# Two attention layers on one NeuronCore, first turn: the last two heads' G in three split passes behind the attention, their operands split during the softmax

## Chip, cores and metric

The kernel runs on one core of one Trainium2 chip. The time is the device time of one execution in microseconds; the median of three runs of the kernel before is 1091.12 us (1090.59 to 1092.88).

## The reference

128 graphs of 64 nodes with 256 features go through two layers. The first is a masked multi-head attention with 8 heads of 32, an output projection and a layer norm. The second is a graph attention with four heads:

```
Wh     = einsum(h, W) + bW            # 4 heads, 256 x 256 each
e      = einsum(Wh, attn)
A_mat  = tanh(where(adj, einsum(e, Wh), 0))
hp     = relu(einsum(A_mat, Wh))
ha, hf = concat(hp) @ A_w.T, h @ fc_w.T
coeff  = sigmoid(hf @ g1_w.T + ha @ g2_w.T + gbias)
out    = layernorm(h + hf * coeff + ha * (1 - coeff))
```

Since W and attn are constant, the scores of a head are h G h^T with G = W^T attn^T W. The kernel computes G once for each head: first M (a product of attn and W), then G from M and W. It also needs W transposed.

## The kernel before

The 128 graphs are 16 groups of 8. A turn takes group A through the first layer and group B = A - 1 through the second, interleaved on each engine; turn 0 has only the first layer of group 0 and the preparation of the weights, and a last turn only the second layer. Turns 2 to 14 are a loop, the others are written out. Each of the five engines has its own list of steps in order (the five functions `turn`); an engine does its steps in that order and waits on semaphores between them. So a step that waits holds everything behind it on its engine. SP issues the loads and stores, PE is TensorE, ACT ScalarE, DVE VectorE and POOL GpSimd.

Precision: most matmuls are made of three passes of fp32r operands. A value is split into `_hi`, a copy rounded to fp32r (made by ACT), and `_lo`, the remainder (a subtraction, made by DVE or POOL); lo x hi, hi x lo and hi x hi are added up in PSUM. M and G are computed in plain fp32 instead, for which the trace shows two rows for each matmul, and each result is split afterwards: `G_high` on ACT (L877), `G_low` on DVE (L1108). M1 holds M in SBUF.

PSUM has eight banks. `claim` makes PE wait until the tile that was in a bank before has been taken; `await_tile` makes a reader wait for a bank to be filled. The lists FIRST, BODY and LAST say which tile goes to which bank: G4 to G6 follow G0 to G2 in banks 1 to 3, G7 follows G3 in bank 6.

Steps of turn 0 that matter here, in order:

- PE (L755): queries, keys, scores, M0 to M7 (L419), values, then the transposes of the probabilities (L542) mixed with G0 to G3 (L431), the attention (L560: 128 small matmuls), G4 to G6, the output projection `project` (L382 to L384), G7, the transposes of W (L441), queries of group 1, the gate weights, the transposes of h (L585), keys of group 1.
- ACT (L1022): the M copies (L871) mixed with three of the four exponentials (L911), wo_hi (`out_weight`, L866), the value copies (L907), the probs copies (L916) and G_high(0 to 3), x_hi of group 1 (`x_split`, L827), at_hi (`attention`, L925), then `late(0)`, `late(1)` and `late(2)` (L858: the rounded parts of A_w in two halves and of g2_w) between G_high(4 to 7), then the W copies.
- DVE (L1367): the softmax (`shift`: mask added L1187, maximum L1190, difference L1192; `total`: sum L1197, reciprocal L1200), wo_lo (`early_low(3)`, L1120), `shifted_fc` (L1146, L1148), G_low, at_lo, `residual`, `new_h` (L1271), h's low part.
- POOL (L1518): the mask, `probs_scaled` (L1480: four products by the reciprocals), `x_and_bias` (L1473: y plus the output bias), x_lo of group 1 (L1441), `late(0)` (L1451: aw_lo, 128 x 2048), `root_1` (the inverse deviation of the first norm), the mask of group 1, `h_low` (L1455), `hT_whole` (L1463), `late(1)` (L1451: the low part of g2_w, called g in the trace).

In turn 1 PE computes T0 to T7 of group 0 (hT times G) with the scores of group 1 behind T0, then half of hf, and then `adj_scores` (L615), which waits until ACT has copied T4 to T7. ACT's order there is T0, T1, exponential 0, T2, T3, exponential 1, T4, T5, exponential 2, T6, T7, exponential 3, hf, tanh. Each exponential waits for DVE's difference L1192 of its tile.

Of the kernel before, what the change touches and what calls it, by code (L numbers as in the profile page):

```python
# [5 lines left out]
F32 = mybir.dt.float32  # L6
F32R = mybir.dt.float32r
# [3 lines left out]
ALU = mybir.AluOpType  # L11
# [3 lines left out]
P = 128  # L15
# [43 lines left out]
def stage_kernel(nc, x, xT, adjS, adjT, masks, eye, pair_eye, wq, bq, wk, bk, wv, bv, wo, bo,  # L59
                 Wn, attn, AwT, fcn, g1T, g2T, gb, out):  # L60
    ctx = ExitStack()
    with ctx:
# [26 lines left out]


        Wq, Wk, Wv, Wo = (pair(n, [P, DC, D]) for n in ("wq", "wk", "wv", "wo"))
        Wt = pair("wt", [P, DC, H2 * D])
        G = pair("g", [P, DC, H2 * D])
        FF = pair("ff", [P, DC, 2 * D])
        Aw = pair("aw", [P, KC, D])
# [63 lines left out]
        raw_m = at("raw_m", [P, JB - 1, S], F32, r_U + 18432)  # L159
        w_sum = at("w_sum", [P, DC * H2], F32, r_U + 19200)  # L160
        w_off = at("w_off", [P, DC * H2], F32, r_U + 19232)
        fc_sum = at("fc_sum", [P, DC], F32, r_U + 19264)
        assert base + place[0] <= nc.sbuf_usable_end, (base, place[0], nc.sbuf_usable_end)

# [34 lines left out]
        passed = sem("passed")  # L199
        zeros_ready, end_ready = sem("zeros_ready"), sem("end_ready")  # L200
        neg2, from2_ready, last_stats = sem("neg2"), sem("from2_ready"), sem("last_stats")

        def carried(eng):

# [175 lines left out]
        def _(pe):  # L380
# [42 lines left out]
            def G_products(ns):  # L423
                if 0 in ns:
                    for n in range(4, 8):
                        await_taken(pe, "S", f"M{n}", 0)
                for n in ns:
                    hh, dc = n // DC, n % DC
                    bank = claim(pe, "S", f"G{n}", 0)
                    for pc in range(DC):  # L430
                        ins = pe.matmul(bank[:, 0:D], M1[:, pc, hh, dc * P:dc * P + P],  # L431
                                        W_nat[:, pc * H2 + hh, 0:D], start=pc == 0, stop=pc == DC - 1)
                    filled(ins, "S", f"G{n}", 0)
# [321 lines left out]
            def turn(A, B, more):  # L755
                if B is None:
                    warm_up()
                    first_queries()
                    keys(0)
                    scores(0)  # L760
                    M1_products(range(H2 * DC))
                    values(0, 0)
                    values(0, 1)
                    probs_T(0, range(2))
                    G_products(range(2))
                    probs_T(0, range(2, 3))
                    G_products(range(2, 3))
                    probs_T(0, range(3, JB))
                    G_products(range(3, 4))
                    attention(0, range(DC))  # L770
                    G_products(range(4, 7))
                    project(0)
                    G_products(range(7, H2 * DC))
                    W_transposed()
                    queries(1)
                    gate_weights()
                    h_T(0)
                    keys(1)
                    return
                for n in range(KC):  # L780
                    T_tile(B, n)
                    if A is not None and n == 0:
                        scores(A)
                    if A is None and n == 3:
                        res_T(B - 1)
                h_fc(B, 0)
                adj_scores(B)
                if A is None:
                    h_fc(B, 1)
                    gathered(B)  # L790
                    for s in range(2):
                        gate_h_half(B, s)
                    heads_out(B, range(KC))
                    h_a_half(B, 0, 0)
                    h_a_half(B, 0, 1)
                    h_a_half(B, 1, 0)
                    gate_a_half(B, 0)
                    h_a_half(B, 1, 1)
                    res_T_first(B)
                    gate_a_last(B)  # L800
                    res_T_last(B)
                    return
                values(A, 0)
                values(A, 1)
                probs_T(A, range(JB))
                gathered(B)
                attention(A, range(DC))
                h_fc(B, 1)
                heads_out(B, range(KC // 2))
                project(A)  # L810
                heads_out(B, range(KC // 2, KC))
                h_a(B)
                gate_h(B)
                h_T(A)
                gate_a(B)
                if more:
                    queries(A + 1)
                    keys(A + 1)
                    res_T(B)
# [4 lines left out]
        def _(act):  # L824
# [29 lines left out]
            def late(n):  # L854

                act.wait_ge(late_in, 16 * 2)
                to, raw = ((Aw[0][:, 0:4, :], raw_A[:, 0:4, :]), (Aw[0][:, 4:8, :], raw_A[:, 4:8, :]), (G2[0][:], raw_g2[:]))[n]
                act.activation(to, raw, ACT.Copy).then_inc(late_hi, 1)  # L858

            def masks_in():  # L860
                act.wait_ge(mask_in, 16)
# [160 lines left out]
            def turn(A, B, more):  # L1022
                if B is None:
# [9 lines left out]
                    M1_copies(range(1, 3))  # L1033
                    exps(0, 1)
                    M1_copies(range(3, 6))
                    out_weight()
                    M1_copies(range(6, H2 * DC))
                    exps(0, 2)
                    values(0, 0)
                    exps(0, 3)  # L1040
                    values(0, 1)
                    probs_T(0, range(2))
# [2 lines left out]
                    G_high(range(2, 3))  # L1045
                    probs_T(0, range(3, JB))
                    G_high(range(3, 4))
                    x_split(1, x_second)
                    attention(0)
                    late(0)  # L1050
                    G_high(range(4, 5))
                    late(1)
                    G_high(range(5, 7))
                    late(2)
                    G_high(range(7, H2 * DC))
                    W_high()
                    queries(1)
                    fc_high()
# [47 lines left out]
        def _(dve):  # L1106
# [37 lines left out]
            def shifted_fc():  # L1144
                dve.wait_ge(gate_in, 16 * 2)
                dve.tensor_reduce(fc_sum[:], fc_nat[:], AX.X, ALU.add).then_inc(sum_fc, 1)  # L1146
                dve.wait_ge(sum_fc, 1)
                dve.scalar_tensor_tensor(out=fc_nat[:], in0=fc_sum[:].unsqueeze(2).to_broadcast([P, DC, D]),  # L1148
                                         scalar=-1.0 / D, in1=fc_nat[:], op0=ALU.mult, op1=ALU.add).then_inc(fc_ready, 1)

            def G_low(ns):
                for n in ns:
# [214 lines left out]
            def turn(A, B, more):  # L1367
                if B is None:
# [4 lines left out]
                    shift(0, 1)  # L1373
                    early_low(2, Wv, raw_v)
                    softmax_rest(0)
                    early_low(3, Wo, raw_o)
                    shifted_fc()
                    G_low(range(4))
                    attention(0)
                    G_low(range(4, 7))  # L1380
                    residual(0)
                    G_low(range(7, H2 * DC))
                    W_low(range(2))
                    new_h(0)
                    W_low(range(2, 4))
# [49 lines left out]
        def _(pool):  # L1435
# [82 lines left out]
            def turn(A, B, more):  # L1518
                if B is None:
# [1 line left out]
                    probs_scaled(0)  # L1521
                    x_and_bias(0)
                    x_low(1, x_second)
                    late(0)
                    root_1(0)
                    mask(1)
                    h_low(0)
                    hT_whole(0)
                    late(1)
                    return  # L1530
                if later(B):
# [74 lines left out]
```

## Time and profile before

| | us |
|---|---|
| median of three runs | 1091.12 |
| lowest, highest | 1090.59, 1092.88 |
| the profiled execution | 1093.31 |
| its span in the trace | 1091.5 |
| PE busy in it | 1081.2 (99%) |
| DVE, ACT, POOL busy | 704.5, 544.9, 290.5 |

The span is what the trace covers; the profiled execution took 1.8 us more than its span. Busy time is summed over the whole span and says how loaded an engine is, not when. In the rows below each time is in microseconds from the span's start. A row of the timeline is a start, a duration, the engine, the source line, the operation with its output and inputs, and how many neighbouring instructions of that kind it merges. The granted clock of TensorE is given as a share of its full 2.4 GHz.

### The profile page before, as it was taken

Reading aid. Unit: us, or ns where it says so; the run is one execution under the profiler, and the core shown is the slowest. Engines: PE = TensorE matmul, PEld = TensorE weight load, DVE = VectorE, ACT = ScalarE, POOL = GpSimd, SP = SyncE. Lnnn points to the kernel's source line nnn. Section 1 sums busy time; section 2 is a strip of 40 time slices with the busy share of each in tenths; the row PEclk is TensorE's granted clock in tenths of the full one; section 3 lists DMA queues with packets and bytes.
Section 4 is the critical chain, followed back from the end, with each engine's and each line's share of the span. In section 5 each row is a group of like instructions: output and inputs, shape, how many; then the busy total and the mean of one; then the engine's idle time right before and its main releaser. Section 6 shows DMA issues by size and latency. Waiting matters only on the chain. (4 is left out here: it accounts for less than half of the span.)

```text
span 1091.5 us, 25444 instructions
## 1 busy us (share of the span) xinstructions
PE 1081.2 (99%) x10102; PEld 908.8 (83%) x10102; DVE 704.5 (65%) x1321; ACT 544.9 (50%) x988; POOL 290.5 (27%) x279
## 2 busy tenths in 40 slices
PE   9999999999999999999999999999999999999998
PEld 7788888888888888788888888888888888878887
DVE  7685766666676575765756666575765757666544
ACT  6563553625446373563635446363562735536252
POOL 2442331232322223322232322223322222312200
PEclk9999999999999999999999999999999999999999
DMA  7000100100010000100100010000100001000000
GB/s 263 3 22 22 41 24 20 41 20 19 22 40 22 20 19 22 40 22 20 41 16 24 22 40 22 20 19 22 40 22 20 26 15 39 22 23 22 1 20 20
DMA packets 26590, 32.60 MB, mean 30 GB/s; under 512 B 4161, under 2 KB 23105, under 8 KB 26177
## 3 DMA queue, kind: packets, MB, share of 16 engines
q1 hardware_dynamic: 26128, 31.93, 8.8%
q8 instruction: 21, 0.34, 0.1%
q10 hardware_dynamic: 432, 0.26, 0.1%
q14 instruction: 9, 0.07, 0.0%
HBM read 23.80 MB, written 8.39 MB: 29 GB/s over the span
## 5 line engine op out<-in xcount | busy, mean ns | idle before, releaser
L972 ACT ACTIVATE cat_hi<-bank 128x512 fp32r<-128x512 f32 x128 | 76.6, 598 | 127.0 <-PE bank L395 127.0
L935 ACT ACTIVATE T<-bank 128x512 f32<-128x512 f32 x128 | 75.0, 604 | 86.5 <-PE bank L395 86.4
L1108 DVE SCALAR_TENSOR_TENSOR cat_lo<-bank,cat_hi 128x512 fp32r<-128x512 f32 x128 | 86.5, 685 | 39.0 <-ACT cat_hi L972 37.0
L390 PE MATMUL bank<-hT_hi,g_lo 128*128 128x512 f32 x256 | 102.6, 401 | 0.0
L383 PE MATMUL bank<-cat_hi,aw_lo 128*128 128x512 f32 (+1 forms) x272 | 102.4, 377 | 0.0
L384 PE MATMUL bank<-cat_hi,aw_hi 128*128 128x512 f32 (+1 forms) x272 | 102.4, 377 | 0.0
L382 PE MATMUL bank<-cat_lo,aw_hi 128*128 128x512 f32 (+1 forms) x272 | 102.4, 377 | 0.0
L1480 POOL TENSOR_TENSOR probs<-probs,den 128x512 f32<-128x512 f32 x64 | 67.6, 1057 | 123.9 <-DVE den L1200 122.7
L391 PE MATMUL bank<-U_hi,wt_hi 128*128 128x512 f32 x256 | 99.8, 390 | 0.0
L391 PE MATMUL bank<-hT_hi,g_hi 128*128 128x512 f32 x256 | 99.8, 390 | 0.0
L390 PE MATMUL bank<-U_hi,wt_lo 128*128 128x512 f32 x256 | 99.8, 390 | 0.0
L1108 DVE SCALAR_TENSOR_TENSOR haT_lo<-bank,haT_hi 128x512 fp32r<-128x512 f32 (+1 forms) x34 | 22.4, 660 | 113.2 <-ACT haT_hi L977 106.1
L1473 POOL TENSOR_TENSOR y<-y,bo_all 128x1024 f32<-128x1024 f32 x16 | 38.9, 2434 | 195.4 <-ACT at_hi L925 195.4
L1108 DVE SCALAR_TENSOR_TENSOR U_lo<-bank,U_hi 128x512 fp32r<-128x512 f32 x128 | 78.0, 680 | 12.9 <-ACT U_hi L966 12.9
L977 ACT ACTIVATE haT_hi<-bank 128x512 fp32r<-128x512 f32 x30 | 17.9, 598 | 125.9 <-PE bank L384 125.9
L395 PE MATMUL bank<-U_lo,wt_hi 128*128 128x512 f32 x256 | 78.9, 389 | 0.0
L395 PE MATMUL bank<-hT_lo,g_hi 128*128 128x512 f32 x256 | 78.8, 389 | 0.0
L966 ACT ACTIVATE U_hi<-bank 128x512 fp32r<-128x512 f32 x128 | 64.4, 629 | 8.8 <-PE bank L638 8.8
L1463 POOL TENSOR_TENSOR hT<-hT_hi,hT_lo 128x1024 f32<-128x1024 f32 x16 | 38.8, 2425 | 108.6 <-DVE hT_lo L1108 108.6
L615 PE MATMUL bank<-T,hT 128*64 128x256 f32 x512 | 58.8, 382 | 0.4 <-ACT T L935 0.4
L383 PEld LDWEIGHTS bank<-cat_hi,aw_lo 128*128 128x128 f32 x272 | 51.2, 188 | 9.4
L382 PEld LDWEIGHTS bank<-cat_lo,aw_hi 128*128 128x128 f32 x272 | 51.2, 188 | 9.4
(203 smaller groups left out, 2753.5 us busy)
## 6 DMA issues: line engine op xcount, KB each, us to landing
y<-in_x SPq DMA_DIRECT2D x16, 512.0 KB, 3.6
out<-res SPq DMA_DIRECT2D x15, 512.0 KB, 3.0
x_raw<-in_xT SPq DMA_DIRECT2D x14, 512.0 KB, 3.4
W_nat<-in_Wn SPq DMA_DIRECT2D x1, 1028.0 KB, 7.8
adjS_u<-in_adjS SPq DMA_DIRECT2D x16, 64.0 KB, 3.0
attn_nat<-in_attn SPq DMA_DIRECT2D x1, 1024.0 KB, 9.0
raw_A<-in_AwT SPq DMA_DIRECT2D x1, 1024.0 KB, 8.9
x_second<-in_xT SPq DMA_DIRECT2D x1, 512.0 KB, 10.9
```

The lines of the kernel that those rows point to most:

```text
L382: pe.matmul(out, asel(a[0]), bsel(b[1]), start=first, stop=False)
L383: pe.matmul(out, asel(a[1]), bsel(b[0]), start=False, stop=False)
L384: return pe.matmul(out, asel(a[0]), bsel(b[0]), start=False, stop=last)
L390: pe.matmul(out, wsel(w[1]), dsel(d[0]), start=first and n == 0, stop=False)
L391: pe.matmul(out, wsel(w[0]), dsel(d[0]), start=False, stop=False)
L395: ins = pe.matmul(out, wsel(w[0]), dsel(d[1]), start=False, stop=last and n == len(terms) - 1)
L615: ins = pe.matmul(bank[b * S:b * S + S, q * D:q * D + D].rearrange("p (h n) -> p h n", h=H2), hT[:, k, first:first + S], T[:, k, :, first: ...
L935: take(act.activation(T[:, n % DC, n // DC, :], bank[:], ACT.Copy), "B", f"T{n}", g)
L966: act.activation(U_hi[:, c, :, first:first + P], bank[:].rearrange("p (h t) -> p h t", h=H2), ACT.Copy).then_inc(U_hi_ready, 1)
L972: act.activation(cat_hi[:, n, :], bank[:], ACT.Relu).then_inc(cat_hi_ready, 1)
L1108: return dve.scalar_tensor_tensor(out=out, in0=bank, scalar=bias, in1=hi.bitcast(F32), op0=op, op1=ALU.subtract)
L1480: pool.tensor_tensor(view, view, den[:, j, :].unsqueeze(2).to_broadcast([P, NG, S]), ALU.mult) \
```

## The change

The changed kernel computes G4 to G7 (heads 2 and 3) as three fp32r passes from split copies of M and W, all four behind the attention and ahead of the projection. The split copies M_part and W_part of the two heads lie in the memory of Wt, which is written later. ACT makes the rounded parts (W's where wo_hi was, M's behind the first value copy), DVE the remainders (`parts_low`, where wo_lo was). wo_hi and wo_lo move behind G_high(3) and G_low(3). On ACT x_hi of group 1 goes behind the attention and `late(0 to 2)` behind G_high(7). On POOL `late(0)` moves from behind x_lo to behind `hT_whole`.

```
@@ memory
-        Wt = pair("wt", [P, DC, H2 * D])
+        r_wt = region(16384)
+        Wt = at("wt_hi", [P, DC, H2 * D], F32R, r_wt), at("wt_lo", [P, DC, H2 * D], F32R, r_wt + 8192)
+        W_part = tuple(at(f"W_part{i}", [P, DC, 2, D], F32R, r_wt + 4096 * i) for i in range(2))
+        M_part = tuple(at(f"M_part{i}", [P, DC, 2, D], F32R, r_wt + 8192 + 4096 * i) for i in range(2))
@@ PE, G_products
+                    if n >= H2:
+                        pe.wait_ge(parts_ready, 2)
+                        for pc in range(DC):
+                            ins = product(bank[:, 0:D], M_part, W_part, lambda t: t[:, pc, hh - 2, dc * P:dc * P + P],
+                                          lambda t: t[:, pc, hh - 2, :], pc == 0, pc == DC - 1)
+                        filled(ins, "S", f"G{n}", 0)
+                        continue
@@ PE, turn 0
                     attention(0, range(DC))
-                    G_products(range(4, 7))
+                    G_products(range(4, H2 * DC))
                     project(0)
-                    G_products(range(7, H2 * DC))
@@ ACT
+            def W_part_high():
+                act.wait_ge(W_ready, H2 * DC)
+                act.activation(W_part[0][:], last_heads(W_nat[:, :, 0:D]), ACT.Copy).then_inc(W_part_hi, 1)
+            def M_part_high():
+                for n in range(4, 8):
+                    await_taken(act, "S", f"M{n}", 0)
+                act.activation(M_part[0][:], M1[:, :, 2:4, :], ACT.Copy).then_inc(M_part_hi, 1)
@@ ACT, turn 0
                     M1_copies(range(3, 6))
-                    out_weight()
+                    W_part_high()
                     M1_copies(range(6, H2 * DC))
                     exps(0, 2)
                     values(0, 0)
+                    M_part_high()
                     exps(0, 3)
...
                     G_high(range(3, 4))
+                    out_weight()
+                    attention(0)
                     x_split(1, x_second)
-                    attention(0)
-                    late(0)
-                    G_high(range(4, 5))
-                    late(1)
-                    G_high(range(5, 7))
-                    late(2)
-                    G_high(range(7, H2 * DC))
+                    G_high(range(4, H2 * DC))
+                    for n in range(3):
+                        late(n)
@@ DVE
+            def parts_low():
+                dve.wait_ge(M_part_hi, 1)
+                dve.tensor_tensor(M_part[1][:], M1[:, :, 2:4, :], M_part[0][:].bitcast(F32), ALU.subtract) \
+                   .then_inc(parts_ready, 1)
+                dve.wait_ge(W_part_hi, 1)
+                dve.tensor_tensor(W_part[1][:], W_nat[:, :, 0:D].rearrange("p (o h) d -> p o h d", h=H2)[:, :, 2:4, :],
+                                  W_part[0][:].bitcast(F32), ALU.subtract).then_inc(parts_ready, 1)
@@ DVE, turn 0
                     softmax_rest(0)
-                    early_low(3, Wo, raw_o)
+                    parts_low()
                     shifted_fc()
                     G_low(range(4))
+                    early_low(3, Wo, raw_o)
                     attention(0)
-                    G_low(range(4, 7))
+                    G_low(range(4, H2 * DC))
                     residual(0)
-                    G_low(range(7, H2 * DC))
@@ POOL, turn 0
                     x_low(1, x_second)
-                    late(0)
                     root_1(0)
                     mask(1)
                     h_low(0)
                     hT_whole(0)
+                    late(0)
                     late(1)
```

## Rows read from the trace of the kernel before

**Rows 1.** The page's busy time by engine (busy us, share of span, instructions).

```profile
PE 1081.2 (99%) x10102; PEld 908.8 (83%) x10102; DVE 704.5 (65%) x1321; ACT 544.9 (50%) x988; POOL 290.5 (27%) x279
```

**Rows 2.** Waits of PE: line, what released it, total us, times, longest.

```profile
PE bank L560 <- issue: 2.1, 1, 2.1
...
PE bank L529 <- issue: 1.0, 1, 1.0
```

**Rows 3.** Timeline of PE, first turn: start, duration, line, operation, count.

```profile
27.50 0.66 PE L542 MATMUL bank<-ident,probs 128*128 128x128 f32 x4
...
28.95 1.17 PE L560 MATMUL bank<-PT,v 64*32 64x64 f32 x96
...
32.23 0.46 PE L560 MATMUL bank<-PT,v 64*32 64x64 f32 x32 [2.10 <-issue]
...
32.62 4.54 PE L431 MATMUL bank<-W_nat,M 128*128 128x256 f32 x12
...
36.81 0.47 PE L382 MATMUL bank<-wo_lo,at_hi 128*128 128x256 f32 x1
...
39.86 1.02 PE L431 MATMUL bank<-W_nat,M 128*128 128x256 f32 x4
...
40.73 1.91 PE L441 MATMUL bank<-ident,W_nat 128*128 128x128 f32 x16
...
47.38 1.04 PE L585 MATMUL bank<-ident,y 128*128 128x128 f32 x8
```

**Rows 4.** Windows: length, busy by engine, then PEclk, DMA share, GB/s (last three).

```profile
29.75:30.00 0.25, 0.25 (x37) 0.21 (x25) 0.15 (x1) 0.25 (x1) 0.25 (x1) 1.00 0.23 66
...
33.50:33.75 0.25, 0.25 (x2) 0.19 (x1) 0.04 (x1) 0.25 (x2) 0.00 (x0) 0.50 0.25 66
```

**Rows 5.** Windows around the low clock, and around the stop near 975.

```profile
32.50:36.50 4.00, 4.00 (x36) 3.16 (x14) 2.08 (x5) 3.66 (x8) 0.31 (x1) 0.57 0.02 6
...
974.00:976.00 2.00, 1.10 (x99) 0.96 (x80) 0.00 (x0) 0.36 (x1) 1.55 (x4) 1.00 0.00 0
```

**Rows 6.** Timeline of ACT, first turn.

```profile
24.08 0.63 ACT L911 ACTIVATE probs<-probs 128x512 f32<-128x512 f32 x1 [1.19 <-DVE probs L1192]
```

**Rows 7.** Timeline of DVE, turns 0 and 1.

```profile
25.58 0.96 DVE L1120 TENSOR_TENSOR wo_lo<-raw_o,wo_hi 128x512 fp32r<-128x512 f32 x1
...
44.94 1.38 DVE L1271 TENSOR_SCALAR y<-y,from,rstd 128x256 f32<-128x256 f32 x4 [0.65 <-POOL from L1492]
...
55.47 1.98 DVE L1192 TENSOR_TENSOR probs<-probs,mx 128x512 f32<-128x512 f32 x1
...
58.81 1.46 DVE L1192 TENSOR_TENSOR probs<-probs,mx 128x512 f32<-128x512 f32 x1
...
62.41 0.69 DVE L1192 TENSOR_TENSOR probs<-probs,mx 128x512 f32<-128x512 f32 x1
```

**Rows 8.** Timeline of POOL, turns 0 and 1.

```profile
22.11 1.04 POOL L1480 TENSOR_TENSOR probs<-probs,den 128x512 f32<-128x512 f32 x1 [1.79 <-DVE den L1200]
...
24.96 2.49 POOL L1480 TENSOR_TENSOR probs<-probs,den 128x512 f32<-128x512 f32 x2 [1.80 <-DVE den L1200]
...
36.65 4.60 POOL L1451 TENSOR_TENSOR aw_lo<-raw_A,aw_hi 128x2048 fp32r<-128x2048 f32 x1 [3.84 <-ACT aw_hi L858]
...
54.51 2.40 POOL L1455 TENSOR_TENSOR h_lo<-y,h_hi 128x1024 fp32r<-128x1024 f32 x1
...
56.86 2.86 POOL L1463 TENSOR_TENSOR hT<-hT_hi,hT_lo 128x1024 f32<-128x1024 f32 x1
...
59.67 1.74 POOL L1451 TENSOR_TENSOR g_lo<-raw_g,g_hi 128x512 fp32r<-128x512 f32 x1
```

**Rows 9.** Timeline of ACT, turn 1.

```profile
63.14 0.63 ACT L911 ACTIVATE probs<-probs 128x512 f32<-128x512 f32 x1 [1.23 <-DVE probs L1192]
...
63.68 1.06 ACT L935 ACTIVATE T<-bank 128x512 f32<-128x512 f32 x2
```

**Rows 10.** Timeline of PE, turn 1.

```profile
65.10 3.67 PE L615 MATMUL bank<-T,hT 128*64 128x256 f32 x32
```

More of the change, by code:

```diff
@@ L201, in stage_kernel @@
         neg2, from2_ready, last_stats = sem("neg2"), sem("from2_ready"), sem("last_stats")
+        W_part_hi, M_part_hi, parts_ready = sem("W_part_hi"), sem("M_part_hi"), sem("parts_ready")
         def carried(eng):
@@ L858, in late, with last_heads @@
                 act.activation(to, raw, ACT.Copy).then_inc(late_hi, 1)
+            def last_heads(t):
+                return t.rearrange("p (o h) d -> p o h d", h=H2)[:, :, 2:4, :]
+            def W_part_high():
[5 more added lines that the diff above has]
+                act.activation(M_part[0][:], M1[:, :, 2:4, :], ACT.Copy).then_inc(M_part_hi, 1)
             def masks_in():
```

## The prediction, made before the changed kernel was run

> **What bounds the kernel now.** I read the page's busy times first: TensorE (PE) is busy for 1081.2 of 1091.5 us, so what counts is when PE stands still, runs at its lower clock, or has less to do [rows 1]. The list of PE's waits then shows how few stops there are: 2.1 us in front of an L560 matmul (attention) and 1.0 us at L529 (scores) are the largest behind the start [rows 2]. The timeline of PE puts the 2.1 us into the first turn: 96 of 128 L560 matmuls, nothing from 30.12 to 32.23, then the other 32; no engine is named as releaser ("issue"), and the only transfer near it is one of 66 GB/s over 29.75 to 30.00, 16 KB, which I take for instructions [rows 3, 4]. Last, the windows give the clock: about half a microsecond after PE resumed it fell from 2.4 to 1.2 GHz and came back at 36.1. The mean granted clock of 32.5 to 36.5 is 0.57 of full: 2 x (1 - 0.57) x 4.0 = 3.4 us at half rate, which cost 1.7 us of PE work [rows 5]. The changed G products ran almost wholly in that stretch.
>
> **G's last four tiles (gain).** Before, each of the eight matmuls of G4 to G7 (two per tile, plain fp32) is two rows of the trace. Twelve rows take 32.62 to 36.81 = 4.19 us, the last four 39.86 to 40.73 = 0.87 us: 5.06 us [rows 3]. Afterwards there are 4 x 2 x 3 = 24 fp32r matmuls of 256 columns, the form of the output projection, whose starts are 0.12 us apart at 2.4 GHz (24 in 3.05 us with the first, slower step) [rows 3]. At 1.2 GHz no such row exists; bounds are 0.12 (no slowing) and 0.24 (all of it), and I take 0.24, since the twelve G rows before took 0.35 us each there and the last four 0.22. With the clock's times moved as below: one matmul at full rate, 14.3 in the 3.4 us at half rate, 8.8 at full rate, 4.6 us in all. Change: -0.5 us (from -2.2 with no slow clock to 0).
>
> **The parts split in the softmax's shadow (loss).** On ACT the 1.05 us copy of W's part takes the place of wo_hi (0.62) among the M copies; the M copy behind it, at 20.00, starts 0.4 us later and is still done when the last M bank comes at 20.86. The copy of M's part fits in the 1.19 us that ACT idled ahead of the exponential at 24.08 [rows 6]. On DVE it is different. DVE and POOL do not overlap when both read two SBUF tensors. wo_lo started at 25.58 and took 0.96 us, where the same form takes 0.69; POOL's probs product takes 1.04 when free (22.11), so the one of 24.96 ended at 26.00, and 0.55 us of DVE work followed. The next POOL product, due at 26.00, ended at 27.45: 1.49 us instead of 1.04 [rows 7, 8]. Now M_part_lo stands where wo_lo stood, with 1024 elements for 512: 2 x 0.55 = 1.1 us from 26.0. POOL's fourth product ends at 26.0 + 1.1 + 1.04 = 28.1 instead of 27.5. PE's last four probs transposes, at 27.50 and in front of G3 and the attention, wait for just this product [rows 3]. Loss: +0.64 us (bounds 0 and 0.7; 0 if the instruction stop behind it ends at a fixed time). W_part_lo comes behind that product (28.1 to 29.2), POOL's y plus bias behind W_part_lo (to 31.6), fc_nat's difference behind that (32.2), G_low(0 to 3) by 33.5. PE reaches G4 at 32.62 + 0.64 = 33.26 and wants G0's bank, free at 32.5, then one more bank per tile: no wait, and its new wait for parts_ready is over at 29.2. wo_lo (34.1) is long ready for the projection.
>
> **G7 ahead of the projection, the moved splits on ACT and POOL (nothing in turn 0).** The projection starts at 37.8 instead of 36.81, so y1 and the DVE, POOL, DVE chain behind it come 1.0 us later: h ready at 47.3 instead of 46.3 [rows 7]. PE gets to h's transposes at 47.38 + 0.14 = 47.5 [rows 3]; 1.06 us of slack become 0.2. The at_hi copies are no later than PE, x_hi of the next turn is done at about 36.1 and x_lo at 38.5, with queries(1) at 42.4 on PE. The Aw and G2 copies (2.8 us on ACT) now fill 38.1 to 40.7, before W0 is there. If the 0.2 us are too little, PE waits for what is missing.
>
> **late(0) on POOL, behind hT_whole (the large loss).** The 4.60 us product aw_lo leaves 36.65, where nothing on DVE needed the port (its work there reads PSUM), and lands behind hT, which ends at 59.7 [rows 8]. h_low, for which SP's next x load waits, and hT stay ahead of it; g_lo and the four probs products of turn 1 stand behind it, the last done by 72.7, before PE's transposes want it. There DVE runs the second turn's softmax. Its L1192 subtraction reads two SBUF tensors. Row 55.47 took 1.98 us and ended 0.54 us after POOL's h_low (54.51 + 2.40 = 56.91); row 58.81 took 1.46 us and ended 0.55 us after hT (59.72); the free ones take 0.69 [rows 7, 8]. So aw_lo, due at 59.67, first waits 0.57 us for that second subtraction (as g_lo did: 1.74 us), and holds until 59.67 + 0.57 + 4.60 = 64.84. The third subtraction, at 62.41, then ends at 65.39 instead of 63.10: +2.3 us [rows 7]. Behind it on ACT queue the exponential (63.14), T6 and T7 (until 64.74), and PE's adjacency scores need T7's copy at 65.10: a slack of 0.36 us [rows 9, 10]. PE stands still for 2.3 - 0.36 = 1.95 us (bounds 0 and 2.5; the upper one if the fourth subtraction, due at 67.7, also loses to a POOL product, A_hi then reaches ACT so late that the copy of v0, which frees the bank of the third probs transpose, costs 0.5 more).
>
> The Trainium skill (SBUF — State Buffer, section "Who interferes with whom") says that the port pair of VectorE and GpSimd is an exclusive lock, held for the whole instruction by whoever issues first. If the port were instead shared by bandwidth, the subtraction would lose about its own 0.55 us, nearly covered by the slack, and the change would cost nothing here. The rows above (1.98 and 1.46 us, each ended by POOL's end) agree with the lock; no row shows a DVE instruction behind one as long as 4.6 us.
>
> **The clock after that stop.** The one stop of 2.1 us was followed by 3.4 us at 1.2 GHz; the stop of 1.0 us near 975 was not (clock 1.00) [rows 2, 5]. 1.95 us is nearest to the first, so I take the fall: +1.7 us (bounds 0 and 1.7).
>
> **Instruction positions.** G4 to G7 issue 16 more PE instructions net, so every later fetch point moves by them. Of the kernel's 32 bursts of short matmuls (scores and attention, 16 each) two held such a stop, of 2.1 and 1.0 us [rows 2]; I take 0, bounds -1.0 (the second stop gone) and +1.0 (one more like it).
>
> Sum: -0.5 + 0.64 + 1.95 + 1.7 = +3.8 us. The profiled execution took 1093.31 us for a span of 1091.5 and would take 1097.1. It lies 2.2 us above the median of the runs, 1091.12; against that median I forecast 1094.9 us.
>
> **Rivals.**
> A. The lock holds but the clock does not fall, since the stop is a little shorter than the one that had that result: -0.5 + 0.64 + 1.95 (to 2.5) = +2.1 to +2.6, 1093.2 to 1093.7. For it: one precedent only on each side. Against: 1.95 is nearly 2.1.
> B. aw_lo does not reach PE: the third subtraction gets in before it, or POOL's order is shifted by a microsecond. Then -0.5 + 0.64 = about 0, 1091.2. Against: POOL's queue is in order and aw_hi has been ready for 20 us.
> C. Faster: the first turn's 2.1 us stop is set by when its instructions arrive and not by when PE gets there. Then the 0.64 us of waiting come out of the stop, which shrinks to 1.5 us, and the clock does not fall (it decides between 1.0 and 2.1). All 24 passes run at 0.12: 2.9 instead of 5.06 us, -2.2. With B's absence of the port stop this gives 1088.9; with the port stop it gives 1090.9 (+1.95, clock full). Against: the fetch appears to follow PE's own progress, since the next 16 KB moved (33.50 to 33.75) 1.4 us after PE had resumed [rows 4].
> D. The change does less than it says: the 24 passes cost no less than the 16 rows (0 instead of -0.5). 1095.4, inside the forecast's own spread.
>
> **How the numbers follow.** Forecast with the clock's fall (D in it) 0.45, A 0.27, B 0.14, C 0.14. A measurement of this kernel can tell 0.2% (2.2 us) from no change, so the borders are 1088.9 and 1093.3. Slower: the forecast's 0.43 and half of A, 0.56. Faster: the better half of C, 0.07. The rest, 0.37, is the same. Range 1090.6 to 1096.0: its top is the forecast with the 0.5 of the v0 copy and 0.6 of a new short stop, its bottom leaves out only half of C and a little of B. The likeliest case alone spans 1093.9 to 1096.0.
>
> **What would show it.** Right: PE idle in front of L615 of about 2 us near 66, released by ACT's T copy; an L1192 row of about 3 us there, beside a POOL aw_lo row of about 5.2; clock 0.50 for some 3 us behind it; probs T3 transposes 0.6 us late; G4 to G7 in one block of 4.6 us. Wrong: an unlengthened third L1192, a clock of 1.00 at 68 to 71 (then A), or an attention stop well under 2.1 us (then C).

## The result

The changed kernel takes 1094.16 us in the median of 17 runs (1092.61 to 1096.91), the kernel before 1090.47 us in 17 runs beside them (1088.35 to 1094.22). The ratio is 1.0039, interval 1.0029 to 1.0049: slower by 4.2 us by the ratio (3.2 to 5.3), and by 3.7 us from median to median. The forecast was +3.8 us, or 1094.9 us. The kernel before spreads over 6 us by itself, and most of that goes with a stop of PE that only some executions have (below); so beside each median the lowest time is of use, since it compares the least disturbed executions: 1092.61 against 1088.35 is +4.3 us.

In the changed kernel the source lines are others: L1223 is L1192 of before (the softmax's subtraction), L628 is L615 (adjacency scores), L573 is L560 (attention), L1482 is L1451 (aw_lo, g_lo), L598 is L585 (h's transposes), L555 is L542 (probs transposes), L387 to L389 are L382 to L384 (the three passes of a product), L1131 is L1108 (the remainders), L413 is L408 (a wait of the last turn that both kernels have), L959 the copies of T (L935).

The list of PE's waits of the changed kernel (total us, times, longest) already holds the answer to [rows 2] (one row of 0.2 us is left out):

```profile
PE bank L628 <- ACT T L959: 2.5, 2, 2.2
PE bank L413 <- POOL hf L1467: 1.3, 1, 1.3
PE bank L387 <- DVE g_lo L1131: 1.3, 1, 1.3
PE bank L555 <- POOL probs L1511: 0.4, 1, 0.4
PE bank L387 <- DVE at_lo L1131: 0.2, 1, 0.2
```

The two stops of before, at attention and at scores of a late turn, are gone from this execution; in their place PE waits 2.2 us for a copy of T, 1.3 us for G_low and 0.6 us in small pieces. The timelines of DVE and POOL in turn 1 show what is behind the first; they answer to [rows 7, 8]:

```profile
53.42 1.99 DVE L1223 TENSOR_TENSOR probs<-probs,mx 128x512 f32<-128x512 f32 x1
...
56.76 1.46 DVE L1223 TENSOR_TENSOR probs<-probs,mx 128x512 f32<-128x512 f32 x1
...
60.36 2.88 DVE L1223 TENSOR_TENSOR probs<-probs,mx 128x512 f32<-128x512 f32 x1
...
65.40 1.53 DVE L1223 TENSOR_TENSOR probs<-probs,mx 128x512 f32<-128x512 f32 x1
```

```profile
52.45 2.41 POOL L1486 TENSOR_TENSOR h_lo<-y,h_hi 128x1024 fp32r<-128x1024 f32 x1
54.80 2.87 POOL L1494 TENSOR_TENSOR hT<-hT_hi,hT_lo 128x1024 f32<-128x1024 f32 x1
57.63 5.06 POOL L1482 TENSOR_TENSOR aw_lo<-raw_A,aw_hi 128x2048 fp32r<-128x2048 f32 x1
62.64 1.73 POOL L1482 TENSOR_TENSOR g_lo<-raw_g,g_hi 128x512 fp32r<-128x512 f32 x1
```

The third subtraction is issued at 60.36, while aw_lo holds the port from 57.63 (its first half microsecond waits for the second subtraction) until 62.69. It ends at 63.24, 0.55 us after that, instead of after 0.69 us. The exponential, T6 and T7 follow it on ACT until 64.87, and PE's scores start at 65.24 with 2.17 us of idle time before them. The windows (last three columns: PEclk, DMA share, GB/s) show that the clock fell to half in this execution: (1 - 0.57) x 2 x 4 = 3.4 us at half rate, the length of [rows 5].

```profile
63.81 1.06 ACT L959 ACTIVATE T<-bank 128x512 f32<-128x512 f32 x2
```

```profile
62.46 0.62 PE L400 MATMUL bank<-hT_lo,ff_hi 128*128 128x512 f32 x2
65.24 5.36 PE L628 MATMUL bank<-T,hT 128*64 128x256 f32 x32 [2.17 <-ACT T L959]
```

```profile
64.00:66.00 2.00, 0.76 (x8) 0.66 (x10) 1.93 (x4) 0.88 (x2) 2.00 (x3) 1.00 0.00 0
66.00:70.00 4.00, 4.00 (x25) 2.85 (x23) 3.60 (x6) 1.71 (x3) 2.42 (x3) 0.57 0.00 0
```

Turn 0 of the same execution, first DVE, then PE. They answer to [rows 3, 7]:

```profile
25.41 1.50 DVE L1176 TENSOR_TENSOR M_part<-M,M_part 128x1024 fp32r<-128x1024 f32 x1
26.82 2.06 DVE L1179 TENSOR_TENSOR W_part<-W_nat,W_part 128x1024 fp32r<-128x1024 f32 x1
28.81 0.67 DVE L1169 TENSOR_REDUCE fc_sum<-fc_nat 128x2 f32<-128x512 f32 x1
29.51 2.15 DVE L1171 SCALAR_TENSOR_TENSOR fc_nat<-fc_sum,fc_nat 128x512 f32<-128x512 f32 x1
31.59 1.41 DVE L1131 SCALAR_TENSOR_TENSOR g_lo<-bank,g_hi 128x256 fp32r<-128x256 f32 x4
```

```profile
26.41 1.03 PE L444 MATMUL bank<-W_nat,M 128*128 128x256 f32 x4
27.86 0.66 PE L555 MATMUL bank<-ident,probs 128*128 128x128 f32 x4 [0.42 <-POOL probs L1511]
...
29.31 1.48 PE L573 MATMUL bank<-PT,v 64*32 64x64 f32 x128
32.05 0.39 PE L387 MATMUL bank<-W_part,M_part 128*128 128x256 f32 x1 [1.26 <-DVE g_lo L1131]
...
34.91 0.28 PE L389 MATMUL bank<-W_part,M_part 128*128 128x256 f32 x1
35.42 0.35 PE L387 MATMUL bank<-wo_lo,at_hi 128*128 128x256 f32 x1 [0.23 <-DVE at_lo L1131]
```

Here all 128 attention matmuls run in one piece, so PE is at G4 at 30.8 and not at 33.3. The bank of G0 is free only when G_low(0) has run, and that stands on DVE behind three instructions that waited for POOL (1.50, 2.06 and 2.15 us where the bare work is 1.1, 1.1 and 0.55). The 24 passes then take 32.05 to 35.03 (the last start and one step of 0.12) = 2.98 us at full clock.

The idle times in brackets are shorter than what a wait costs, since a matmul row lasts beyond the start of the next (the passes are 0.28 us long and start 0.12 us apart). From start to start the costs come out larger. The probs transposes start 1.45 us after the G2 rows ahead of them, where e5 below needs 0.86; G4 starts 2.74 us after the attention, where e9 below needs 1.41; the projection starts 0.51 us after the last pass, instead of 0.12; the scores of L628 start 2.78 us after the last hf rows, and those of the kernel before 0.59. So the four waits cost 0.59, 1.33, 0.39 and 2.19 us, where the brackets say 0.42, 1.26, 0.23 and 2.17. The rows for comparison, of e5, of e9 and of the kernel before:

```profile
26.59 1.03 PE L431 MATMUL bank<-W_nat,M 128*128 128x256 f32 x4
27.45 0.60 PE L542 MATMUL bank<-ident,probs 128*128 128x128 f32 x4
```

```profile
29.41 1.48 PE L573 MATMUL bank<-PT,v 64*32 64x64 f32 x128
30.82 0.38 PE L387 MATMUL bank<-W_part,M_part 128*128 128x256 f32 x1
```

```profile
64.51 0.61 PE L395 MATMUL bank<-hT_lo,ff_hi 128*128 128x512 f32 x2
```

### The profile page after: what moved, and what is told of

It is laid out like the page before. It is cut to its first block and busy times, and to the rows that moved or that the text cites. A ratio compares the mean times of both kernels' runs of the same rounds, so it can differ in the third digit from the quotient of the medians.

```text
span 1092.2 us, 25470 instructions
## 1 busy us (share of the span) xinstructions
PE 1080.7 (99%) x10110; PEld 908.8 (83%) x10110; DVE 713.9 (65%) x1323; ACT 546.7 (50%) x990; POOL 291.2 (27%) x279
## 5 line engine op out<-in xcount | busy, mean ns | idle before, releaser
L959 ACT ACTIVATE T<-bank 128x512 f32<-128x512 f32 x128 | 75.0, 603 | 85.5 <-PE bank L400 85.5
L1131 DVE SCALAR_TENSOR_TENSOR cat_lo<-bank,cat_hi 128x512 fp32r<-128x512 f32 x128 | 86.5, 686 | 39.0 <-ACT cat_hi L996 37.0
L389 PE MATMUL bank<-cat_hi,aw_hi 128*128 128x512 f32 (+1 forms) x272 | 102.6, 377 | 0.0
L387 PE MATMUL bank<-cat_lo,aw_hi 128*128 128x512 f32 (+1 forms) x272 | 102.5, 377 | 0.0
L1131 DVE SCALAR_TENSOR_TENSOR haT_lo<-bank,haT_hi 128x512 fp32r<-128x512 f32 (+1 forms) x34 | 22.4, 660 | 113.1 <-ACT haT_hi L1001 106.0
L1131 DVE SCALAR_TENSOR_TENSOR U_lo<-bank,U_hi 128x512 fp32r<-128x512 f32 x128 | 78.0, 682 | 12.9 <-ACT U_hi L990 12.9
L628 PE MATMUL bank<-T,hT 128*64 128x256 f32 x512 | 60.5, 390 | 2.5 <-ACT T L959 2.5
L387 PEld LDWEIGHTS bank<-cat_lo,aw_hi 128*128 128x128 f32 x272 | 51.2, 188 | 9.4
```

The costliest lines, as they stand in the source:

```text
L387: pe.matmul(out, asel(a[0]), bsel(b[1]), start=first, stop=False)
L389: return pe.matmul(out, asel(a[0]), bsel(b[0]), start=False, stop=last)
L628: ins = pe.matmul(bank[b * S:b * S + S, q * D:q * D + D].rearrange("p (h n) -> p h n", h=H2), hT[:, k, first:first + S], T[:, k, :, first: ...
L959: take(act.activation(T[:, n % DC, n // DC, :], bank[:], ACT.Copy), "B", f"T{n}", g)
L1131: return dve.scalar_tensor_tensor(out=out, in0=bank, scalar=bias, in1=hi.bitcast(F32), op0=op, op1=ALU.subtract)
```

## The experiments

All ran in three groups of four, each beside runs of the kernel before. Ratios are to the kernel before, with their 95% intervals; "lowest over before" is the kernel's lowest time less the lowest of before in its group (1088.76, 1088.46 and 1088.31 us; 1088.35 for the changed kernel).

| kernel | runs | median | lowest over before | ratio |
|---|---|---|---|---|
| changed | 17 | 1094.16 | +4.3 | 1.0039 (1.0029 to 1.0049) |
| e1 late(0) back | 12 | 1093.07 | +2.2 | 1.0014 (1.0001 to 1.0028) |
| e2 late(0) only | 12 | 1094.81 | +2.4 | 1.0031 (1.0016 to 1.0045) |
| e3 shifted_fc later | 12 | 1093.12 | +2.4 | 1.0020 (1.0006 to 1.0034) |
| e4 aw_lo in four | 12 | 1091.63 | +2.3 | 1.0005 (0.9993 to 1.0018) |
| e5 order only | 12 | 1091.33 | +0.9 | 1.0013 (0.9999 to 1.0026) |
| e6 = e1 and e3 | 12 | 1090.23 | +0.9 | 1.0006 (0.9993 to 1.0019) |
| e7 parts behind G | 11 | 1091.44 | +2.2 | 1.0015 (1.0005 to 1.0026) |
| e8 changed, again | 6 | 1096.35 | +5.7 | 1.0054 (1.0039 to 1.0069) |
| e9 = e3, late(0) in POOL's gap | 12 | 1090.02 | +0.2 | 1.0014 (1.0001 to 1.0026) |
| e10 = e9, softmax's tail freed | 12 | 1089.00 | 0.0 | 1.0003 (0.9992 to 1.0014) |
| e11 = e10, attention split | 12 | 1090.12 | +1.4 | 1.0004 (0.9993 to 1.0015) |
| e12 before, attention split | 12 | 1090.72 | +1.6 | 1.0010 (0.9997 to 1.0023) |

**e1, late(0) back.** The change without its move on POOL.

```
@@ POOL, turn 0, against the changed kernel
                     x_low(1, x_second)
+                    late(0)
                     root_1(0)
...
                     hT_whole(0)
-                    late(0)
```

> The changed kernel, but POOL's late(0) (aw_lo) stands where it stood before the change, behind x_lo of group 1. Theory (port): aw_lo on POOL in turn 1 holds the port against the third L1192-type subtraction; that cost 2.2 us of PE standing still and 1.7 us of low clock behind it. Without it the third subtraction takes 0.7 us, PE does not wait for T7's copy, the clock stays full around 66 to 70, and the time is 3.5 to 4 us under the changed kernel's 1094.2: about 1090.4, ratio to before about 1.000. Rival (the DVE chain of turn 0, parts_low and shifted_fc behind the port, is the main cost): at most 1 us is gained, ratio 1.003.

The lowest time fell by 2.1 us, the ratio from 1.0039 to 1.0014: this is the larger of the two losses, though less than the 3.5 to 4 us that I expected with the clock's fall in every execution. The stop is gone; of PE's waits in this kernel the 1.3 us for g_lo is left, and h's transposes have a new one:

```profile
PE bank L387 <- DVE g_lo L1131: 1.3, 1, 1.3
PE bank L555 <- POOL probs L1511: 0.5, 1, 0.5
PE bank L628 <- ACT T L959: 0.4, 1, 0.4
PE bank L598 <- DVE y L1302: 0.3, 1, 0.3
```

**e2, late(0) only.** The same edit the other way round, on the kernel before.

```
@@ POOL, turn 0, against the kernel before
                     x_low(1, x_second)
-                    late(0)
                     root_1(0)
...
                     hT_whole(0)
+                    late(0)
```

> The kernel before, with one edit: POOL's late(0) moved behind hT_whole, as in the change. Port theory: the same stop of about 2 us in front of the adjacency scores of turn 1, with the clock's fall in most executions: ratio to before 1.003 to 1.004 (+3 to +4 us), the third subtraction about 2.9 us long. Rival (the stop needs the new parts' work as well): ratio 1.000, no long subtraction.

One moved instruction makes +2.4 us in the lowest time and 1.0031. The third subtraction and PE's stop:

```profile
62.52 2.89 DVE L1192 TENSOR_TENSOR probs<-probs,mx 128x512 f32<-128x512 f32 x1
```

```profile
67.40 0.87 PE L615 MATMUL bank<-T,hT 128*64 128x256 f32 x6 [2.14 <-ACT T L935]
```

The clock did not fall behind it in this execution (window 68 to 72):

```profile
68.00:72.00 4.00, 4.00 (x38) 3.09 (x34) 3.40 (x6) 1.98 (x4) 2.53 (x3) 1.00 0.00 0
```

**e4, aw_lo in four.** This tells a held port from a shared one.

```
@@ POOL, late(n)
+                if n == 0:
+                    for i in range(4):
+                        k = slice(2 * i, 2 * i + 2)
+                        ins = pool.tensor_tensor(w[1][:, k, :], raw[:, k, :], w[0][:, k, :].bitcast(F32), ALU.subtract)
+                    ins.then_inc(late_ready, 1)
+                    return
```

> The changed kernel, with aw_lo on POOL as four instructions of 128 x 512 in place of one of 128 x 2048, in the same place. Theory (exclusive port, held for an instruction): the third subtraction waits for one piece at most (1.2 us), ends 0.3 to 1.2 us late instead of 2.2, PE's stop in front of the adjacency scores is 0 to 0.9 us and the clock stays full; time about 1091, ratio 1.000 to 1.001. Rival (port shared by bandwidth, or POOL as a whole has priority): the subtraction takes as long as with one instruction, ratio 1.004.

The same elements in the same place, and the third subtraction takes 0.81 us instead of 2.88; aw_lo as a whole gets longer:

```profile
63.16 0.81 DVE L1223 TENSOR_TENSOR probs<-probs,mx 128x512 f32<-128x512 f32 x1
```

```profile
60.43 5.94 POOL L1485 TENSOR_TENSOR aw_lo<-raw_A,aw_hi 128x512 fp32r<-128x512 f32 x4
66.34 1.72 POOL L1488 TENSOR_TENSOR g_lo<-raw_g,g_hi 128x512 fp32r<-128x512 f32 x1
68.02 5.40 POOL L1517 TENSOR_TENSOR probs<-probs,den 128x512 f32<-128x512 f32 x4
```

PE's wait for T's copy is 0.4 us, as in the kernel before, and the ratio 1.0005. The lowest time is still 2.3 us above that of before, since the waits of turn 0 are left. A port shared by bandwidth is ruled out: the work of both engines is unchanged, only the length of one instruction is. The Trainium skill (SBUF — State Buffer, section "Who interferes with whom") calls the shared port pair an exclusive lock, which is the rule that the prediction weighed. The runs agree with it, 2.88 against 0.81 us.

**e3, shifted_fc later.** The second loss.

```
@@ DVE, turn 0, against the changed kernel
                     parts_low()
-                    shifted_fc()
                     G_low(range(4))
                     early_low(3, Wo, raw_o)
                     attention(0)
                     G_low(range(4, H2 * DC))
+                    shifted_fc()
                     residual(0)
```

> The changed kernel, with shifted_fc on DVE moved from ahead of G_low(0 to 3) to behind G_low(7). Theory: PE's 1.3 us in front of G4, released by DVE's G_low, is the wait for bank 1 behind fc_nat's difference (2.15 us, most of it waiting for POOL's y plus bias): it goes, and with it most of the 0.2 us in front of the projection; time 1.0 to 1.5 us under the changed kernel's, about 1092.9, ratio 1.0025. Rival (the wait is parts_ready, whose remainders end at 28.8, or PE's instruction supply): the wait stays, ratio 1.004.

The lowest time fell by 1.9 us, the ratio to 1.0020, and the wait for g_lo is not in its list. (In its profiled execution the attention had a stop of 2.4 us, which alone would hide that wait, as it does in e8; e6, e9 and e10 have the same edit, and e9 and e10 are without such a stop and without the wait.)

**e5, order only.** The new order with the old work.

```
@@ against the kernel before; PE, turn 0
                     attention(0, range(DC))
-                    G_products(range(4, 7))
+                    G_products(range(4, H2 * DC))
                     project(0)
-                    G_products(range(7, H2 * DC))
```

In words: on ACT x_split goes behind the attention, and G_high(4 to 7) ahead of late(0 to 2); on DVE G_low(4 to 7) goes ahead of the residual.

> The kernel before with the order of the change and none of its new work: G4 to G7 stay plain fp32 and stand ahead of the projection, x_hi of group 1 behind the attention, late(0 to 2) on ACT behind G_high(7), G_low(4 to 7) ahead of the residual; wo_hi, wo_lo and POOL's late(0) stay where they were. Theory (the parts' work on DVE is what the first turn pays for, the order is free): ratio to before 0.9995 to 1.0005, no PE wait for g_lo, at_lo or probs. Rival (the order itself eats slack, at h's transposes or at the projection): 0.5 to 1 us slower, a wait in front of L382 or L585 or of their like.

The rival was right: +0.9 us in the lowest time, and PE waits 0.8 us in front of h's transposes. POOL's timeline says why: ACT now makes aw_hi later, aw_lo ends at 43.23, and only then can POOL begin the root of the first norm, whose input DVE had ready at about 41.9.

```profile
38.63 4.60 POOL L1446 TENSOR_TENSOR aw_lo<-raw_A,aw_hi 128x2048 fp32r<-128x2048 f32 x1 [0.89 <-ACT aw_hi L857]
43.20 0.24 POOL L1481 TENSOR_SCALAR var<-mv 128x4 f32<-128x4 f32 x1
```

```profile
46.60 1.09 PE L585 MATMUL bank<-ident,y 128*128 128x128 f32 x8 [0.80 <-DVE y L1267]
```

So in the new order the move of late(0) bought 0.8 us (0.3 in e1) and cost 2.1 us and more. This run also prices the passes: the plain G4 to G7 at full clock take 32.52 to 35.89 = 3.37 us, the 24 passes 2.98: 0.4 us saved.

```profile
32.52 3.72 PE L431 MATMUL bank<-W_nat,M 128*128 128x256 f32 x16
35.89 0.47 PE L382 MATMUL bank<-wo_lo,at_hi 128*128 128x256 f32 x1
```

**e6, both losses taken away** (e1's and e3's edits together).

> The changed kernel with both edits: shifted_fc behind G_low(7) and POOL's late(0) back behind x_lo. Theory (the two losses are separate and add up): no wait for g_lo in front of G4, no stop in front of the adjacency scores; what is left is 0.4 us for the probs product and the 0.6 us that the passes save; ratio to before 0.9995 to 1.0005, its fastest executions about 1.5 us under those with late(0) back alone (1090.9). Rival (aw_lo, now in turn 0, delays the first norm's root or fc_nat's difference): a wait in front of h's transposes takes back 0.5 to 1 us.

+0.9 us in the lowest time, 1.0006. The two losses add up, and the rival's wait is there as well: 0.8 us at h's transposes, as in e5, beside 0.5 us for the probs product, less the 0.4 us that the passes save.

**e7, parts behind G.** late(0) back as in e1, and on DVE:

```
                     softmax_rest(0)
-                    parts_low()
                     shifted_fc()
                     G_low(range(4))
+                    parts_low()
```

> The changed kernel with POOL's late(0) back, and on DVE parts_low behind G_low(0 to 3) in place of ahead of shifted_fc. Theory: POOL's fourth probs product is not held by M's remainder any more, so the 0.4 us in front of the last probs transposes go; but the two remainders now wait for POOL's y plus bias and end near 32.2, so PE waits for them in front of G4 where the attention ran without a stop: about 1.8 us there, the same sum, ratio 1.001 to 1.0015. Rival (the remainders hide in either place): no wait in front of G4, ratio 1.000.

As expected, the wait only changes its name; +2.2 us as in e1:

```profile
32.54 0.36 PE L387 MATMUL bank<-W_part,M_part 128*128 128x256 f32 x1 [1.88 <-DVE W_part L1179]
```

**e8, the changed kernel again.**

> The changed kernel once more, beside the others and with a second profile. Theory: the stop of 2.1 to 2.2 us in front of the adjacency scores is in every execution; whether the clock falls behind it, and whether the attention of turn 0 stops for 2 us or PE waits 1.3 us for g_lo instead, changes from execution to execution. Ratio 1.003 to 1.0045. Rival (the stop is not in every execution): a profile without it, near 1092.

Six runs, 1094.16 to 1096.70, ratio 1.0054, whose interval overlaps that of the first comparison. Its profile has the stop in front of L628 (2.14 us), and the attention's stop as well (2.07 us, and then no wait for g_lo), and half clock behind both.

**e9, late(0) in POOL's gap.** e3's edit, and on POOL:

```
                     root_1(0)
+                    pool.wait_ge(h_ready, NP)
+                    late(0)
                     mask(1)
                     h_low(0)
                     hT_whole(0)
-                    late(0)
                     late(1)
```

> The changed kernel with shifted_fc behind G_low(7), and with POOL's late(0) behind root_1 and a wait for all four h_ready, ahead of the mask of group 1: there POOL stood idle for 8 us and DVE has no instruction with two SBUF inputs for about 5 us. Theory: aw_lo costs nothing there: no stop in front of the adjacency scores (2.1 us), none in front of h's transposes (0.8 us with late(0) back in turn 0's middle); left are the probs product's 0.4 us and the passes' 0.6 us gain; ratio to before 0.999 to 1.000, fastest executions near 1088.6. Rival (something there needs the port: h's normalisation or the ff remainder): a wait at L598 or a later k tile, ratio 1.001.

aw_lo runs from 43.73 to 48.36, costs nothing, and the third subtraction is back at 0.69 us. The complete list of PE's waits:

```profile
PE bank L413 <- POOL hf L1467: 1.3, 1, 1.3
PE bank L555 <- POOL probs L1511: 0.4, 1, 0.4
PE bank L628 <- ACT T L959: 0.4, 1, 0.4
```

Its lowest time is 0.2 us over that of before, near what I expected; the ratio of 1.0014 is not (0.999 to 1.000), since six of its twelve runs lie between 1091.2 and 1093.7 us, against 11 of the 35 of before in this group above 1090.5.

**e10, the softmax's tail freed.** As e9, and the sum of shifted_fc ahead of parts_low, its subtraction behind G_low(7), POOL's y plus bias behind wo_lo:

```
@@ DVE
                     softmax_rest(0)
+                    fc_total()
                     parts_low()
...
+                    fc_shift()
                     residual(0)
@@ POOL, x_and_bias(0)
+                    pool.wait_ge(weights_ready, 4)
```

> As the one before, and on DVE the sum of shifted_fc first, parts_low behind it (so that POOL's fourth probs product is not held), the rest of shifted_fc behind G_low(7); POOL's y plus bias waits for wo_lo (weights_ready 4). Theory: the 0.4 us in front of the last probs transposes go too, and only the 0.6 us of the passes are left as a difference: fastest executions near 1088.2, ratio 0.9990 to 0.9998, too little to tell from no change unless both losses were real. Rival: y plus bias now comes too late for the residual, a wait at h's transposes, ratio 1.000 to 1.001.

The wait for probs is gone, as the theory said, and the rival's wait came, 0.6 us in front of h's transposes, so that the gain of the passes does not show. Lowest times equal, ratio 1.0003 (0.9992 to 1.0014). No version of the change beats the kernel before.

**e11 and e12, the attention split by G3** (e10, and the kernel before):

```
-                    G_products(range(3, 4))
-                    attention(0, range(DC))
+                    attention(0, range(1))
+                    G_products(range(3, 4))
+                    attention(0, range(1, DC))
```

> As the one before, with G3 moved between the two halves of turn 0's attention on PE. Theory (the stop within the attention comes when 256 short instructions are used up before the next 16 KB have arrived, at a time set by when they were asked for): the 0.9 us of G3 come out of the stop, 1.2 to 1.7 us instead of 2.1 to 2.6 in the executions that have it, the clock falls less often; median 0.5 to 1.5 us lower. Rival (the stop follows PE's position in the code): the same stop of 2.1 us or more, the same median.

> The kernel before, with G3 moved between the two halves of turn 0's attention and nothing else. Theory (arrival of instructions): the same fastest executions as before (1088.5 to 1089), but the slow ones 1 to 2.5 us less slow, ratio 0.999. Rival (position in the code): ratio 1.000, a stop of 2.1 us in the profile if the execution has one.

The expectation held for the stop of e11's one profile and failed for the median, which is 1.1 us above that of e10. In e11 the stop sits at the same matmul (the 97th) and lasts 1.3 us instead of 2.1 to 2.6, with a full clock behind it, but a second one of 0.7 us appears ahead of the attention's first matmul:

```profile
29.23 0.85 PE L573 MATMUL bank<-PT,v 64*32 64x64 f32 x64 [0.73 <-issue]
31.07 0.45 PE L573 MATMUL bank<-PT,v 64*32 64x64 f32 x32
32.82 0.46 PE L573 MATMUL bank<-PT,v 64*32 64x64 f32 x32 [1.30 <-issue]
```

The second one is no stop of the same kind, although the profile names no engine for it: the attention needs the last copy of the transposed probabilities, which ACT has done at 29.13, and PE starts at 29.23. G3 used to stand in that gap and covered the copy. e12 has the same 0.73 us (29.21, the copy done at 29.11), and 0.4 us for at_lo in front of the projection. So the edit pays for what it covers, and part of the rise is explained by this wait.

e11's times lie between 1089.7 and 1092.0, where those of before lie between 1088.3 and 1094.0, and its lowest time is 1.4 us above that of before. e12's lowest is 1.6 us above, where I had expected none; its profile has no stop inside the attention, so it says nothing on the length of one. One of its twelve executions took 2737.61 us, for which no profile exists.

## Why the prediction was right, and where it was not

**late(0) on POOL (forecast 1.95 us, measured 2.19).** Right in mechanism, and close in size: the subtraction 2.88 us (forecast 3.0), aw_lo 5.06 us (5.2), PE released by T7's copy. The slack of 0.36 us that I subtracted was not there. In the kernel before the copy ends at 64.74 and PE starts at 65.10 [rows 9, 10]; in the changed one it ends at 64.87 and PE starts at 65.24. So 0.36 us is the way from the copy to PE, which already followed the copy before, and PE is late by the whole lengthening of the subtraction (2.88 - 0.69 = 2.19 us). Shown from both sides by e1 and e2, and the port as its cause by e4. The fourth subtraction did lose to a POOL product (1.53 us), which I had as the upper bound, but cost PE nothing.

**The clock (forecast 1.7 us).** In the profiled execution it came out as written, 3.4 us at half rate. As a step it was mis-sized: of the four profiles with a stop of 2.1 to 2.2 us there, two (changed, e8) had the fall and two (e2, e3) had not. Rival A is what those two were. The mean granted clocks of the 17 runs fit this: the five fastest (1092.61 to 1093.07 us) have 0.999, the other twelve 0.996 to 0.998, and one fall takes about 0.0016 off the mean. They do not say behind which stop a fall came. It should have been counted at about half.

**The attention's stop, taken as part of the kernel.** This was the wrong premise. The profile of before had it (2.10 us and a half clock behind), and I summed against it. Of the eleven executions profiled afterwards, not counting the two that split the attention, six had it (2.07 to 2.65 us) and five had not; the changed kernel's own had not. It comes and goes in the same code, in both kernels. In the profile of before, the stop (2.1), the slow clock behind it (1.7) and the stop near 975 (1.0) make 4.8 of the 5.0 us by which that execution lies above the lowest time; so most of the spread goes with such stops. Rival C had seen that it might depend on when instructions arrive, but as a property of the change. With it absent, my -0.5 us for the passes was -0.4 us (3.37 to 2.98), and not -2.2: the -2.2 set full clock after against half clock before. Where stop and slow clock are there (e4, e6, e8) the 24 passes take 4.4 to 4.5 us, near my 4.6; a pass at half clock takes 0.21 us, and not the 0.24 that I took.

**G0's bank (forecast: no wait; measured 1.33 us, and 0.39 us for at_lo).** I had G0's bank free at 32.5 and G_low done by 33.5, and let PE come at 33.3 because of the stop. Both DVE times were right to half a microsecond; PE came at 30.8. The cover was a stop that half of the executions do not have. e3 shows what it costs without the cover (1.9 us in the lowest time).

**Parts in the softmax's shadow (forecast 0.64, measured 0.59 us).** Right in mechanism and size.

**The order (forecast 0, slack of 0.2 us).** Right in the changed kernel, where nothing stood in front of h's transposes, but for another reason than I gave: late(0) had left the place ahead of root_1. With late(0) there the order costs 0.3 to 0.8 us (e1, e5, e6).

The balance for an execution without the attention's stop, with the costs taken from start to start: 2.19 + 1.33 + 0.39 + 0.59 - 0.4 = 4.1 us of the 4.3 us between the lowest times. The experiments take it away in steps: both losses away +0.9 (e6), late(0) in the gap +0.2 (e9).

That the total came out near is in part luck. The forecast lacked 1.7 us of waits (G0's bank and at_lo), which come only in executions without the attention's stop (e8 has the stop and not the waits). It counted 1.7 us of slow clock in full, which comes in about half. The two misses had opposite signs and nearly the same size.

## What to carry to other kernels

In these runs a subtraction or product of two SBUF tensors on GpSimd was a closed gate for every such instruction on VectorE for its whole length: before one is moved, look for what VectorE runs in the new place, and cut it or put it where VectorE reads PSUM. A stop in one profile may be missing in the next execution; before work is called hidden behind it, compare the lowest times of several runs with the profiled one. The idle time that a profile gives ahead of a row is not the whole price of a wait: compare starts, in two kernels. Where three instructions change places at once, run the order without the work: here it showed that one move paid for another.

## What the runs showed of the hardware

- Within the attention of turn 0 PE stops at the 97th of 128 short matmuls in about half the executions of the same code, for 2.07 to 2.65 us, with no engine to wait for. In e11, with 0.9 us of long matmuls ahead of the place, the stop lasted 1.3 us.
- The stop goes with the time at which 16 KB move on an instruction queue (q8), which the windows of 0.25 us show in all fourteen profiles. That it waits for instructions to arrive fits this well, but no run moved the transfer by itself; what sets its time is open.

| profiles | window in which the 16 KB begin to move, after the attention's first matmul | the 97th matmul |
|---|---|---|
| before, e2, e3, e4, e5, e6, e8 | 0.6 to 0.9 us | stops, goes on 2.5 to 3.0 us after that window's start |
| e11 | 0.8 us | stops for 1.3 us, goes on 2.8 us after that window's start |
| e12 | -0.2 us (before it) | no stop |
| changed, e1, e7, e9, e10 | -3.9 to -6.8 us (before it) | no stop |

- Eleven stops of 2.07 us or more on PE stand in the profiles of all kernels, and the clock fell to half behind seven of them, for 3.4 us each time [rows 5]. Behind the shorter ones (1.9 us in e7, 1.30 in e11, 1.26 in the changed kernel, 1.0 near 975 in [rows 5]) it did not. The same stop in the same place can go either way: 2.07 us (e8) and 2.10 (before) had the fall, 2.11 (e5) and 2.40 (e3) had not.
